# Rows of the first edge kind selected by matmul instead of gathered, and logit weights spread by matmul, in a graph layer on one core

## What is computed

```python
feat = concatenate([h[edge_src], h[edge_dst]], axis=1)      # 8448 edges
e_hh = relu(feat[:128] @ W_hh + b_hh)                       # first kind: 128 edges
e_oo = relu(feat[128:768] @ W_oo + b_oo)                    # 640 edges
e_ho = relu(feat[768:] @ W_ho + b_ho)                       # 7680 edges
logit = concatenate([e_hh, e_oo, e_ho]) @ W_a + b_a         # W_a: 1024 weights
alpha = softmax of logit over the edges with the same edge_dst
z = segment_sum(alpha * h[edge_src], edge_dst)
x = x + relu(concatenate([h, z]) @ W_hn or W_on + bias)     # rows 0..63, rows 64..255
```

## Time and profile before

| what | us |
|---|---|
| median of 3 runs | 320.19 |
| the profiled execution | 319.85 |
| its span | 317.8 |
| PE busy | 306.4 |
| DVE busy | 255.8 |
| ACT busy | 174.4 |
| POOL busy | 154.5 |

### The profile page before, as it was taken

How to read it: one execution, slowest core, us unless ns; L and a number is a source line. 1 busy time by engine, 2 the same in 40 slices (tenths; PEclk the granted TensorE clock), 3 DMA queues, 4 the chain that set the end, 5 groups by cost and what they waited for, 6 DMA issues and landing times.

```text
span 317.8 us, 4204 instructions
## 1 busy us (share of the span) xinstructions
PE 306.4 (96%) x1394; PEld 194.1 (61%) x1399; DVE 255.8 (81%) x442; ACT 174.4 (55%) x437; POOL 154.5 (49%) x149
## 2 busy tenths in 40 slices
PE   8899999999979899999999999999999998999995
PEld 3687688656646667566566666575744645456443
DVE  4775448490799999999979999979898798998164
ACT  3892351573067775648966655865338675493102
POOL 3140027305877778778757877468778600000000
PEclk9999999999999999999999999999999999999999
DMA  6999999999999999999999999999999999999604
GB/s 194 418 425 416 399 427 366 419 424 415 402 405 411 410 407 414 411 410 412 419 419 406 413 415 407 418 418 410 413 413 413 411 414 411 395 377 426 244 0 132
DMA packets 29384, 122.04 MB, mean 384 GB/s; under 512 B 3498, under 2 KB 4010, under 8 KB 24628
## 3 DMA queue, kind: packets, MB, share of 16 engines
q0 software_dynamic: 19008, 69.21, 54.5%
q1 hardware_dynamic: 9236, 48.38, 38.1%
q10 hardware_dynamic: 1120, 4.19, 3.2%
HBM read 115.49 MB, written 6.29 MB: 383 GB/s over the span
## 4 chain that ended last, share of the span: by engine, by line
PE 51%; DMA 20%; DVE 10%; POOL 8%; issue 6%; ACT 4%; SPq 0%; DVEq 0%; ACTq 0%; POOLq 0%
PE psG L1086 17%; PE psG L959 14%; DMA Gp<-p_ho,ids 9%; PE psA L996 5%; DMA q_ho<-T 4%; PE psW L996 4%; POOL Gq L428 3%; DMA q_oo<-T 3%; DVE Gp L737 3%; POOL Gp L414 3%; DMA Gq<-q_ho,ids 2%; PE psG L1163 2%; PE psB L996 2%; PE psG L1056 2%; ACT RL L547 2%
## 5 line engine op out<-in xcount | busy, mean ns | idle before, releaser
L1086 PE MATMUL psG<-W,hT 128*128 128x512 f32 x192 | 84.9, 593 | 0.0
L414 POOL DMA_INDIRECT Gp<-p_ho,ids x60 | 64.1, 1068 | 42.5 <-DMA p_ho<-T 21.4
L737 DVE TENSOR_TENSOR Gp<-Gp,Gq 128x1024 f32<-128x1024 f32 x57 | 69.6, 1220 | 16.6 <-DMA Gq<-q_ho,ids 11.1
L428 POOL DMA_INDIRECT Gq<-q_ho,ids x56 | 65.9, 1178 | 31.3 <-issue 16.8
L741 DVE SCALAR_TENSOR_TENSOR Gp<-Gp,wa 128x1024 f32<-128x1024 f32 x65 | 79.2, 1219 | 0.6
L1086 PEld LDWEIGHTS psG<-W,hT 128*128 128x128 f32 x192 | 35.3, 190 | 39.1 <-issue 39.1
L537 ACT ACTIVATE RW<-ohs,ewh 128x256 fp32r<-128x256 f32 x66 | 33.1, 502 | 34.4 <-DVE ohs L728 28.4
L996 PE MATMUL psW<-RW,ohd 128*128 128x256 f32 x264 | 44.2, 290 | 0.0
L996 PE MATMUL psA<-RL,ohd 128*128 128x256 f32 x240 | 35.4, 291 | 4.3 <-ACT RL L547 3.7
L996 PEld LDWEIGHTS psW<-RW,ohd 128*128 128x128 f32 x264 | 36.3, 189 | 2.9 <-issue 2.9
L996 PEld LDWEIGHTS psA<-RL,ohd 128*128 128x128 f32 x240 | 30.4, 189 | 9.3 <-ACT RL L547 8.2
(11 more groups left out here) (187 smaller groups left out, 393.0 us busy)
## 6 DMA issues: line engine op xcount, KB each, us to landing
W<-weights SPq DMA_DIRECT2D x30, 1024.0 KB, 8.5
Gq<-weights SPq DMA_DIRECT2D x2, 1024.0 KB, 9.3
Gp<-weights SPq DMA_DIRECT2D x4, 512.0 KB, 8.7
Gp<-weights SPq DMA_DIRECT2D x2, 1024.0 KB, 11.8
xs<-x SPq DMA_DIRECT2D x4, 256.0 KB, 3.6
W<-weights SPq DMA_DIRECT2D x2, 512.0 KB, 6.7
h_rows<-h SPq DMA_DIRECT2D x1, 1024.0 KB, 9.0
pre_f<-weights SPq DMA_DIRECT2D x1, 1024.0 KB, 9.9
```

The costliest lines, as they stand in the source:

```text
L414: nc.gpsimd.indirect_dma_start(out=Gp[:, i % NP, :], out_offset=None, in_=p_oo if t <= OO_TILES else p_ho, in_offset=bass.IndirectOffsetOn ...
L428: nc.gpsimd.indirect_dma_start(out=q_place[Q_PLACE[i]], out_offset=None, in_=q_oo if t <= OO_TILES else q_ho, in_offset=bass.IndirectOffse ...
L737: nc.vector.tensor_tensor(Gp[:, i % NP, :], Gp[:, i % NP, :], q_place[Q_PLACE[i]], ALU.add).then_inc(s_sum, 1)
L1086: last = nc.tensor.matmul(psG[:, 2 * t + half, :], hT[:, k, t * P:(t + 1) * P], W[:, s, half * HALF:(half + 1) * HALF], start=u != 1 and k ...
```

## The change

Tile 0's rows are no longer gathered. ACT makes a f32r high part hh_h of h, row tile by row tile, and DVE the low part hh_l (h minus hh_h). After the fifth chunk PE spreads the 128 source ids and the 128 destination ids of tile 0 over all partitions, by two f32 matmuls of the ids (weights, one column repeated) with the identity, into psB. DVE compares them with the node number of each partition (node, made by POOL): hots, a 0/1 matrix of 128 x 256 for each of the two row tiles of h. In the places of the four lots of transposes PE multiplies each 128 x 128 square of hh_h and hh_l with hots, eight f32r matmuls of 128 x 256 a lot, so that psB holds the chosen rows already transposed, source and destination side by side. ACT's copy to hsT takes them in that new order.

The logit weights are loaded as one row of 4 KB, ahead of the bias rows in SP's queue, and spread by two f32 matmuls of a row of ones with them, into psA and psW; ACT copies the two banks to wa. The clears of the two banks move behind the thirteenth chunk. h is still stored to DRAM, since it is read again at the end, but POOL waits for it only before the third p gather, whose slot holds h; it waits there for the low part of h too, and before the eighth p gather, whose slot holds hh_h, for the last of the selection matmuls (before: the tenth).

```diff
-        _, hs = shared(("gp_low", [P, NP - 2, D], f32), ("hs", [P, 2, D], f32))
+        _, hh_h, hh_l = shared(("gp_low", [P, H_PLACE, D], f32), ("hh_h", [P, NT, D], f32r), ("hh_l", [P, NT, D], f32r))
@@ SP
             sp.dma_start(ew[:, :], edge_w).then_inc(s_ew, 16)
+            sp.dma_start(war[:, :], w_a).then_inc(s_wa, 16)
...
                     load_pre(1)
-                    sp.dma_start(wa[:, :], w_a.broadcast_to((P, D))).then_inc(s_wa, 16)
@@ POOL
+            nc.gpsimd.iota(node[:, :], pattern=[[P, NT]], base=0, channel_multiplier=1,
+                           allow_small_or_imprecise_dtypes=True)
             pool.wait_ge(s_ids, 16)
-            pool.wait_ge(s_hst, 16)
-            for c in range(2):
-                nc.gpsimd.indirect_dma_start(out=hs[:, c, :], out_offset=None, in_=h_rows,
-                                             in_offset=bass.IndirectOffsetOnAxis(ap=ids[:, 0, c:c + 1], axis=0)
-                                             ).then_inc(s_hg[c], 16)
...
-                elif i == NP - 2:
+                elif i == NT:
+                    pool.wait_ge(s_hst, 16)
+                    pool.wait_ge(s_hhl, NT)
+                elif i == H_PLACE:
                     pool.wait_ge(s_hsT, 4)
@@ ACT
-            highs(6, KC + 2)
+            def rows_high(t):
+                nc.scalar.copy(hh_h[:, t, :], h[:, t, :]).then_inc(s_hhh, 1)
+
+            highs(6, KC)
+            act.wait_ge(s_wab, 1)
+            for half, bank in enumerate((psA, psW)):
+                nc.scalar.copy(wa[:, half * HALF:(half + 1) * HALF], whole(bank)).then_inc(s_wac, 1)
...
+            rows_high(0)
+            high(KC)
+            rows_high(1)
+            high(KC + 1)
             evac_even(0)
@@ DVE
                 if k == 2:
                     evac_odd(0)
                 low(KC + k)
+                if k == 0:
+                    dve.wait_ge(s_idb, 1)
+                    for t in range(NT):
+                        nc.vector.tensor_scalar(hots[:, t, :], psB[:, 0, 0:2 * P], node[:, t:t + 1], None, ALU.is_equal
+                                                ).then_inc(s_hot, 1)
+                if k < NT:
+                    dve.wait_ge(s_hhh, k + 1)
+                    nc.vector.tensor_tensor(hh_l[:, k, :], h[:, k, :], hh_h[:, k, :].bitcast(f32), ALU.subtract
+                                            ).then_inc(s_hhl, 1)
@@ PE
                 if k == 4:
                     pe.wait_ge(s_hTf, 4)
-                    clear(whole(psW))
-                    clear(whole(psA))
+                    pe.wait_ge(s_idf, 1)
+                    for c in range(2):
+                        last = nc.tensor.matmul(psB[:, 0, c * P:(c + 1) * P], idf[:, 0, c:c + 1].broadcast_to((P, P)),
+                                                ident[:, :], start=True, stop=True, skip_group_check=True)
+                    last.then_inc(s_idb, 1)
+                    pe.wait_ge(s_wa, 16)
+                    for half, bank in enumerate((psA, psW)):
+                        last = nc.tensor.matmul(whole(bank), unit[0:1, 0:1].broadcast_to((1, P)),
+                                                war[0:1, half * HALF:(half + 1) * HALF], start=True, stop=True,
+                                                skip_group_check=True)
+                    last.then_inc(s_wab, 1)
...
                 if r < 4:
-                    if r % 2 == 0:
-                        pe.wait_ge(s_hg[r // 2], 16)
-                    if r >= 2:
+                    if r == 0:
+                        pe.wait_ge(s_hhl, NT)
+                        pe.wait_ge(s_hot, NT)
+                    elif r >= 2:
                         pe.wait_ge(s_hsTc, r - 1)
-                    for q in range(4):
-                        kk = 4 * (r % 2) + q
-                        last = nc.tensor.transpose(psB[:, r % 2, q * P:(q + 1) * P],
-                                                   hs[:, r // 2, kk * P:(kk + 1) * P], ident[:, :])
+                    terms = [(t, part) for t in range(NT) for part in (hh_h, hh_l)]
+                    for kk in (2 * r, 2 * r + 1):
+                        for n, (t, part) in enumerate(terms):
+                            last = nc.tensor.matmul(psB[:, r % 2, kk % 2 * N:(kk % 2 + 1) * N],
+                                                    part[:, t, kk * P:(kk + 1) * P], hots[:, t, :],
+                                                    start=n == 0, stop=n == len(terms) - 1, skip_group_check=True)
                     last.then_inc(s_hsT, 1)
+                elif r == 4:
+                    pe.wait_ge(s_wac, 2)
+                    clear(whole(psW))
+                    clear(whole(psA))
```

More of the change, by code:

```diff
@@ L50 @@
 NQ = 8
+H_PLACE = NP - 2 * NT
 RING = 9
@@ L204, in gnn_block @@
         pre_f, = shared(("pre_f", [P, 3, D], f32))
+        war, = shared(("war", [1, D], f32))
         inv_few = sb("inv_few", [P, 2, NT, N], f32)
@@ L213, in gnn_block @@
         ohs = sb("ohs", [P, RING, N], f32r)
+        hots, = shared(("hots", [P, NT, 2 * P], f32r))
         A = sb("A", [P, NT, N], f32)
+        node = sb("node", [P, NT], f32)
         den = sb("den", [P, NT], f32)
@@ L240, in gnn_block @@
         s_idf = sem("ids_as_float")
-        s_hst, s_hg = sem("h_stored"), [sem("hsrc_in"), sem("hdst_in")]
+        s_hst, s_hhh, s_hhl = sem("h_stored"), sem("h_rows_high"), sem("h_rows_low")
+        s_idb, s_hot = sem("first_ids_spread"), sem("first_hots_made")
+        s_wab, s_wac = sem("wa_spread"), sem("wa_copied")
         s_tab = [sem("p_ho_stored"), sem("q_ho_stored"), sem("p_oo_stored"), sem("q_oo_stored")]
@@ L514, in _ @@
             nc.scalar.copy(selr[:, :], sel[:, :]).then_inc(s_bh, 1)
-            highs(6, KC + 2)
+            def rows_high(t):
[4 more added lines that the diff above has]
+                nc.scalar.copy(wa[:, half * HALF:(half + 1) * HALF], whole(bank)).then_inc(s_wac, 1)
+            act.wait_ge(s_h, 3)
+            act.wait_ge(s_hd, 1)
+            rows_high(0)
+            high(KC)
+            rows_high(1)
+            high(KC + 1)
             evac_even(0)
@@ L520, in _ @@
                 act.wait_ge(s_hsT, r + 1)
-                nc.scalar.copy(hsT[:, r // 2, 4 * (r % 2):4 * (r % 2) + 4, :],
-                               psB[:, r % 2, :].rearrange("p (k e) -> p k e", e=P)).then_inc(s_hsTc, 1)
+                nc.scalar.copy(hsT[:, :, 2 * r:2 * r + 2, :].rearrange("p c k e -> p k c e"),
+                               psB[:, r % 2, :].rearrange("p (k c e) -> p k c e", c=2, e=P)).then_inc(s_hsTc, 1)
             evac_even(1)
@@ L715, in _ @@
                 low(KC + k)
+                if k == 0:
[7 more added lines that the diff above has]
+                                            ).then_inc(s_hhl, 1)
             dve.wait_ge(s_ewh, 1)
             chain(nc.vector.tensor_tensor(ewl[:, :], ew[:, :], ewh[:, :].bitcast(f32), ALU.subtract))
-            dve.wait_ge(s_wa, 16)
+            dve.wait_ge(s_wac, 2)
             dve.wait_ge(s_small, 48)
```

## The result

The changed kernel takes **322.70 us** (median of 4 runs, 322.32 to 322.89) where the kernel before took 319.94 in the same sitting (4 runs): ratio **1.0106, interval 1.0079 to 1.0133**, so 3.4 us slower (2.5 to 4.3). The forecast was 319.3, at most 322.0. The profiled execution took 322.78 us, with a span of 320.8.

The account below looks back on a forecast made before the run. The prediction took full DMA queues as the bound, with PE's order close behind. Bytes -3.8, holes +3.6 and the dent -0.7 gave -0.9 us, PE's +1.0 being covered: median 319.3 us, range 317.2 to 322.0.

Parts of the forecast that it names:

- The bound: Whole kernel: DMA queues hold work all the time (busy share 1.02 from 8 to 298 us), PE's order nearly as decisive.
- the DMA line: All bytes through full queues, one of two lines side by side; its terms were to sum to -0.9 us.
- Bytes: Two gathers and one weight spread, 1.57 MB, leave the queues: -3.8 us at 413 GB/s if queues stay full.
- Ids and spreads: Four f32 matmuls on PE behind the fifth chunk, two with 128 columns and two with 512: +1.1 us.
- The added wait: PE's first bias of the second product waits for DVE's later copy of bank 1: about 0.6 us, 0 to 1.3.
- Selection: 32 f32r matmuls replace 16 transposes in four places on PE before the second product ends: +2.0 us.
- Cover: PE's later waits at 91 and 107 us absorb 2.67 of 3.7 us, two last waits the remaining 1.0.
- Holes: DMA queues run dry near 32 and 40 us, before SP's next loads: 3.6 us together, 1.5 to 5.
- the dent: DMA at 48 to 56 us, 364 GB/s in the kernel before; earlier p gathers fill it, gain taken as 0.7 us.
- The step that failed: Store of q_ho, issued 3.7 us later at 63.8, meets an emptier queue and lands between 70 and 74 us.
- the third: Rival: DVE's operations delay SP's loads up to 60 us, third hole before q_ho lands; 321.5, worst 322.4; chance 0.14.
- The second rival: PE's line takes over between 107 and 240 us and makes the kernel slower: +1.1 us, 321.3 us; chance 0.20.

Follow-up runs that it names:

- pe_after_lot0_b: Kernel before plus 40 bf16 matmuls of zeros on TensorE behind the placing of the first lot, second sitting: 319.19 us for 319.24, ratio 1.0004.
- qho_late_b: Kernel before with ScalarE's two stores of q_ho's left half placed behind five early weight products, second sitting; they came 1.9 and 0.8 us later: ratio 0.9984.
- pe_load_b: Kernel before plus TensorE's added work alone (four f32 matmuls, twenty zero matmuls), all transfers kept, second sitting: 321.65 us for 319.52, ratio 1.0080.
- no_bytes: Kernel before without the 1.57 MB of transfers and no work in their place (some results not the reference's): 317.99 us for 318.85, ratio 0.9962.
- pe_load: Kernel before plus TensorE's added work alone (four f32 matmuls, twenty zero matmuls), all transfers kept, first sitting: 321.89 us for 318.85, ratio 1.0105.
- high8_first: Changed kernel with ScalarE's high parts of chunks 8 and 9 moved ahead of the weight copies and second h tile: 321.68 us, ratio 1.0095 to the kernel before.
- wa_by_dma: Changed kernel with the logit weights spread by DMA again and the clears back in place: 320.43 us, ratio 1.0035 to the kernel before.

## Why the prediction was wrong

- **The bound** was read rightly: the DMA line sets the end, and its lateness at 100 us (2.8) is about the loss (3.0 by the spans, 3.4 by the ratio). That the busy share of 1.02 says the queues are full was too quick: at 76 to 96 us it stays at 1.00 while a tenth of the rate is gone.
- **Bytes, -3.8 us**: wrong as a term by itself. Its condition, queues that stay full, fails not only at 32 us, which I saw, but again before q_ho lands. With nothing else changed 1.57 MB are worth 1.2 us (0.5 to 1.9).
- **Ids and spreads, +1.1 us**: measured 2.45. I read "x16" in the earlier trace rows as sixteen matmuls; it is eight, with two rows each. The Trainium skill's rule (FP8 and Floating Point Precision, TensorE Precision Notes: four passes for true f32) gave 0.9 us for a spread, and the trace of after has 0.95. The rule was right, the row misread, and with 2.45 the forecast of PE's delay would have been 5.1 instead of 3.7.
- **The added wait, 0.6**: measured 0.28. **Selection, +2.0**: right. PE ends the second product 4.2 us later where 3.7 was forecast (3 to 5). The terms as measured would give 4.7; in the trace of the changed kernel PE was already some 0.5 us early at 24 us.
- **Cover**: right in its own terms. The waits at 91 and 107 us are gone, PE is 1.0 us late at 110 (1.0 forecast) and q_oo is stored 0.85 us later. More than right: pe_after_lot0_b hides 4.4 us.
- **Holes, 3.6 us**: 4.8, inside 1.5 to 5. SP's loads came at 33.95 and 40.64 where 33.2 and 39.7 were forecast. The bytes of the first of them flow again 1.6 us after its issue, as counted (1.4 to 2), so the holes were not shortened there. The eighth p gather waits 0.44 us, and the dent's 1.0 us came back.
- **The step that failed**: "And q_ho, issued 3.7 us later at 63.8, finds a queue that is emptier by as much: it lands between 70 and 74". It lands at 76.38. A queue with other work left in it (413 GB/s at 60 to 76 us) doesn't carry a store in its transfer time; the latency only fell from 13.7 to 11.9 us, where the forecast had 6 to 10. I followed PE's delay along PE to 91 us and gave it no price where it enters the queues. That price is 2.3 us, a third hole. The other terms of the DMA line come to +0.1 us where -0.9 was forecast. Of the rivals, the third ("a third hole opens before q_ho lands", 321.5 to 322.4 at the worst) comes nearest, though PE and not VectorE made the hole and it opens behind the landing. The second rival, PE's line, had more of the chances and is refuted by pe_after_lot0_b: it had PE late behind 107 us, and there 4.4 us cost nothing that can be measured.

## What to carry to other kernels

A saved transfer is worth its time only if everything that stands between it and the end is issued as much earlier; otherwise the queue runs dry before the next thing that waits for a result, and most of the saving goes there (1.2 us were left of 3.8 here). The price of work on an engine depends on what is released behind it: follow a delay along every edge out of the engine, stores and slots too, not only along its own waits. To find where queues run thin, cut the stretches finely and read GB/s, not the busy share.

## What the runs showed of the hardware

- An f32 matmul appears as two rows of half its length, so counts of f32 rows are twice those of the program. A 512-column one took 0.95 us one row deep, and a pair of rows in a long run 0.86 (6.87 for sixteen), where an f32r one takes 0.23.
- Over 60 to 64 us, while four f32 matmuls of one row ran (59.33 to 63.70), the granted clock was 0.78, and then 0.50 for 8 us, with TensorE busy all the time; this is one execution. Behind two of them, in the changed kernel, it stayed at 1.00. It fell, too, behind a wait: in the changed kernel to 0.68 over 232 to 236 us, behind the wait of 2.47 us, and pe_after_lot0_b has 0.57 at 92 to 96 us, behind a stretch in which TensorE was busy for 1.63 of 4 us and a wait of 2.37; the kernel before was busy for 2.29 of the same 4 us, waited 1.64 and stayed at 1.00. The ratio of pe_after_lot0_b (1.0004) shows no loss from it.

```profile
88.00:92.00 4.00, 1.63 (x6) 0.56 (x6) 3.93 (x5) 1.96 (x8) 3.08 (x4) 1.00 1.03 406
92.00:96.00 4.00, 3.94 (x21) 3.20 (x20) 3.97 (x6) 3.59 (x9) 3.09 (x4) 0.57 1.00 408
```

- ScalarE's queue issues a DMA before activations that stand ahead of it in the program have run, by ten of them in qho_late_b. The Trainium skill (TensorE: Matmul & The Clock Gate, Architectural detail: the array is 16× 32×32, not 1× 128×128) gives ScalarE's queue eight places, first in, first out; the trace agrees: eight activations stood ahead of the first store, and the second, with ten ahead of it, took 0.72 us instead of 0.33 and ended at 61.58 us, when two of the ten had begun.
- The DMA engines' busy share was 0.99 to 1.01 at 353 to 385 GB/s in pe_load_b, the changed kernel, no_bytes, pe_load and high8_first, and 1.02 to 1.03 at 405 to 411 (in wa_by_dma it did fall, to 0.94 at 358). It hardly tells a full queue from one that is fed at POOL's pace.
